# One program part for cross-attention and experts, with the experts' first work placed in the last output projection

## The chip, the cores and the metric

The kernel runs on one core of a Trainium2 chip. The metric is the device time of one execution in microseconds (us), given as the median of several runs. TensorE (PE) multiplies and transposes, with its weight loads shown apart (PEld); VectorE (DVE), ScalarE (ACT) and GpSimd (POOL) do the elementwise work; SyncE (SP) issues nearly all DMAs. Engines meet only at semaphores.

## The reference

One decoder layer over 4096 tokens (two sequences of 2048) of width 512, in float32:

```
x = x + attn(layernorm(x))            # scores against 2048 fixed keys per head, squared relu, no softmax
x = x + xattn(layernorm(x), ctx)      # 16 heads of 64, 128 context rows a batch, mask, softmax, then Wo
x = x + ffn(layernorm(x))

ffn(x): shared = (silu(x @ sg) * (x @ su)) @ sd                  # 512 -> 1024 -> 512, every token
        e, s   = argmax(x @ gate_w), sigmoid(max(x @ gate_w))    # one of 32 experts
        routed = expert_e(x * s)                                 # the same form, weights of expert e
        return shared + routed
```

Every layernorm needs mean and variance of its 512 numbers per token.

## The kernel before

Products in full float32 precision are made from two halves: each operand is a rounded high part H and a remainder L, and a product is three matmuls, H·H + H·L + L·H (split_matmuls, lines 47 to 49). So whatever goes to PE, weights or activations, is first copied by ACT to the high part, and then DVE subtracts that from the source to get the low part.

Tokens lie in 32 tiles of 128 rows, and 8 groups of 4 tiles (GT = 4, GROUPS = 8). The kernel is a row of program parts ("blocks"). Each has its own program for each engine, and the engines meet at the end of a part, before the next begins: self-attention; the preparation of cross-attention (keys, values, query and output weights); cross-attention proper (lines 645 to 992); the experts (line 1202 on).

Cross-attention proper goes through the 8 groups, with 8 head pairs (steps j = 0 to 7) in each, 64 steps in all. A step is: query, scores, mask, exponentials, normalization by GpSimd (probabilities), transposes of the probabilities (p_transpose), their split by ACT and DVE (t_high, t_low), product with the values (values), and the split of that (a_high, a_low). Steps are staggered: in step n PE makes the scores of n, then the values of n-2 and the transposes of n-1. A finished group is multiplied with the output weights in step 1 of the next group: project(g, i) for tile i, 8 pairs of 3 matmuls each, 24 in all, into the PSUM banks pY0 and pY1 in turn. DVE adds x1, which SP has loaded into xr (add), computes the tile's statistics (out_stats), and SP stores the sum as x2. Within PE's program of the last group, nothing is left to do after p_transpose of step 62; behind the loop come values(62), p_transpose(63), values(63) and then the four projections of the last group (lines 988 to 992).

The experts' part begins with GpSimd's constants, three small conversions on DVE, and the layernorm statistics of all 32 tiles (layernorm_stats, line 489: 32 aggregations and a chain of 15 small operations, each of which waits for the one before). SP loads the router weight rw, the first x2 tiles (xb) and the shared weights. These come in twelve parts of 512 KB: 0 to 3 the gate weight, 4 to 7 the up weight, 8 to 11 the down weight. They pass through a staging tile with three slots (split_weights, lines 453 to 486): part n is loaded when part n-3 has been split, `wait(sp, low_done, n + 1 - SLOTS)`; ACT copies it (high), DVE subtracts (low). The first four tiles are normalized (norm), transposed by PE (x_transpose), copied and subtracted (x_high, x_low), one after another through one PSUM bank, pX.

Then the shared experts run group by group (shared, lines 1332, 1517 and 1678): 8 chunks i of 128 hidden columns, each 12 matmuls of gate, 12 of up; ACT makes the sigmoid, DVE two products and the subtraction, ACT the copy; in chunks 0 and 1 PE adds the router's logits and their transposes. Then four down projections of 24 matmuls. PE starts group 0 when all four tiles are subtracted (xL) and the gate weight is split, the first up matmul when all 8 first parts are (`low_done` 8), and the first down projection when all 12 are. In group 0 the down weight's parts are copied and split in chunks 1, 3, 5 and 7, behind the chunk's own hidden values. After that come the routed experts.

An engine works through its program strictly in the order written, SP too: a DMA behind a waiting one is not issued.

Of the kernel before, what the change touches and what calls it, by code (L numbers as in the profile page):

```python
# [11 lines left out]
NB = 2  # L12
KC = C // P
# [475 lines left out]
def layernorm_stats(nc, link, stats, parts, mv, var, tmp, rstd, mybir):  # L489

    ALU = mybir.AluOpType
    n = stats.shape[1]
    for t in range(n):
        m = nc.vector.bn_aggr(out=mv[:, t, :], in_=stats[:, t, 0:parts, :])
    link(m)
    link(nc.vector.tensor_scalar(var[:, :], mv[:, :, 1], EPS, None, ALU.add))
    rsqrt(nc, link, rstd[:, :], tmp[:, :], var[:, :], ALU, mybir.dt.int32)


def cross_attention(nc, ident, stats, x1, ctx_in, mask, Wq, Wk, Wv, Wo, x2, mybir, bass, ExitStack):  # L500
# [17 lines left out]
    with ExitStack() as keep:  # L518
        sbk = lambda n, s, d=F32: keep.enter_context(nc.sbuf_tensor("b_" + n, s, d))

        kH, kL = (sbk(n, [P, NPAIR, 2, KEYS], F32R) for n in ("kH", "kL"))
        later = [nc.dram_tensor(f"later{n}", (P, NPAIR, KEYS), F32, kind="Internal").ap() for n in "HL"]
        vH, vL = (sbk(n, [KEYS, NB, NPAIR, 2, P], F32R) for n in ("vH", "vL"))
        wqH, wqL = (sbk(n, [P, KC, INNER], F32R) for n in ("wqH", "wqL"))
        woH, woL = (sbk(n, [P, NPAIR, C], F32R) for n in ("woH", "woL"))


        with ExitStack() as ctx:
            sb = lambda n, s, d=F32: ctx.enter_context(nc.sbuf_tensor("b_" + n, s, d))
            ps = lambda n, s: ctx.enter_context(nc.psum_tensor("b_" + n, s, F32))  # L530
            wkH, wkL = (sb(n, [P, KC, INNER], F32R) for n in ("wkH", "wkL"))
            wvH, wvL = (sb(n, [P, KC, INNER], F32R) for n in ("wvH", "wvL"))
            cx = sb("cx", [KEYS, NB, C])
            cH, cL = (sb(n, [P, KC, NB, KEYS], F32R) for n in ("cH", "cL"))
            k1 = [sb(n, [P, 2, KEYS], F32R) for n in ("k1H", "k1L")]
            pC = [ps(f"pC{i}", [P, 2, NB, KEYS]) for i in range(2)]
            pK = [ps(f"pK{i}", [P, NB, KEYS]) for i in range(2)]
            pV = [ps(f"pV{i}", [KEYS, NPAIR // 2, 2, HD]) for i in range(2)]
            s = {n: ctx.enter_context(nc.semaphore("bs_" + n)) for n in
                 "c_in zero ct cH cL k_ps kH kL k_out0 k_out1 v_ps vH vL".split()}  # L540
            parts = []
            for w, hi, lo in ((Wk, wkH, wkL), (Wv, wvH, wvL), (Wq, wqH, wqL)):
                w_v = w.rearrange("(a p) n -> p a n", p=P)
                parts += [(w_v[:, a, :], hi[:, a, :], lo[:, a, :]) for a in range(KC)]
            wo_v = Wo.rearrange("(a p) n -> p a n", p=P)
            parts += [(wo_v[:, a:a + 2, :], woH[:, a:a + 2, :], woL[:, a:a + 2, :]) for a in range(0, NPAIR, 2)]
            load, high, low, low_done = split_weights(nc, ctx, "bs_", parts, mybir)
            block = ctx.enter_context(nc.Block())

            @block.sync  # L550
            def _(sp):
                sp.dma_start(cx[:, :, :], ctx_in.rearrange("b k c -> k b c")).then_inc(s["c_in"], 16)
                load(sp)

            @block.gpsimd
            def _(pool):
                nc.gpsimd.memset(kH[:, :, :, :].bitcast(F32), 0.0).then_inc(s["zero"], 1)
                nc.gpsimd.memset(kL[:, :, :, :].bitcast(F32), 0.0).then_inc(s["zero"], 1)
                nc.gpsimd.memset(vH[:, :, :, :, :].bitcast(F32), 0.0).then_inc(s["zero"], 1)
                nc.gpsimd.memset(vL[:, :, :, :, :].bitcast(F32), 0.0).then_inc(s["zero"], 1)  # L560
                for j in range(NPAIR):
                    pool.wait_ge(s["kL"], j + 1)
                    for part, dst in zip(k1, later):
                        pool.dma_start(dst[:, j, :], part[:, j % 2, :].bitcast(F32)).then_inc(s[f"k_out{j % 2}"], 16)
                for i in range(2):
                    pool.wait_ge(s[f"k_out{i}"], 32 * NPAIR // 2)

            @block.scalar
            def _(act):
                copy = lambda out, in_: nc.scalar.activation(out, in_, ACT.Copy)  # L570
                for i in range(2):
                    act.wait_ge(s["ct"], i + 1)
                    copy(cH[:, 2 * i:2 * i + 2, :, :], pC[i][:, :, :, :]).then_inc(s["cH"], 1)
                high(act, 0, KC)
                act.wait_ge(s["zero"], 2)
                for j in range(NPAIR):
                    high(act, KC + j // 2, KC + (j + 1) // 2)
# [41 lines left out]
            def _(pe):  # L619
                pe.wait_ge(s["c_in"], 16)  # L620
                for a in range(KC):
                    for b in range(NB):
                        m = nc.tensor.transpose(pC[a // 2][:, a % 2, b, :], cx[:, b, a * P:(a + 1) * P], ident[:, :])
                    if a % 2:
                        m.then_inc(s["ct"], 1)
# [1178 lines left out]
```

## Time and profile before

| | us |
|---|---|
| median of 3 runs | 2952.77 (2951.02 to 2953.56) |
| profiled execution, its own time | 2952.46 |
| its span | 2950.8 |
| PE busy | 2813.2 |
| DVE busy | 1788.2 |
| ACT busy | 1599.4 |
| POOL busy | 1027.5 |

The span runs from the first to the last instruction that the profiler recorded; the execution's own time holds a little more than the span. Times inside the trace count from the start of the span. "Idle before" on a row is the time for which the engine had stood still when this instruction began, and behind the arrow stands what it had waited for. The granted clock is a share of full speed; 1.00 is 2.4 GHz and 0.50 is 1.2 GHz.

### The profile page before, as it was taken

The page shows a single profiled execution, that of the slowest core. Times are in us where ns is not written, and L with a number is a line of the kernel's source. Part 1 is how long each engine was busy: PE and PEld are TensorE (multiplying, and loading weights), DVE is VectorE, ACT ScalarE, POOL GpSimd, SP SyncE. Part 2 cuts the span into 40 slices and gives each one's busy share as a digit, 9 for nine tenths or more (in the row PEclk, how much of TensorE's full clock was granted, in tenths as well). Part 3 has the DMA queues.
Part 4 walks back from the last instruction along what each step waited for, and adds up shares of the span by engine and source line. Part 5 has one row for each costly group of instructions (what it writes and reads, how often), then busy time and mean ns, then how long its engine had stood idle before and what let it go on. Part 6 is the DMA issues. An engine that isn't in the chain of part 4 may idle for free. (4 is left out here: it accounts for less than half of the span.)

```text
span 2950.8 us, 46232 instructions
## 1 busy us (share of the span) xinstructions
PE 2813.2 (95%) x13287; PEld 2296.6 (78%) x13289; DVE 1788.2 (61%) x2726; ACT 1599.4 (54%) x2755; POOL 1027.5 (35%) x705
## 2 busy tenths in 40 slices
PE   7999999999779999999969999999999999999998
PEld 5888888888558777777747888887788888888886
DVE  6566665665465566666544443444877864776776
ACT  6888878887545555555522111111465753665665
POOL 5888888888611122221200000000133322332332
PEclk9999999999889999999979999999999999999999
DMA  1000000000320111111031111121888873876885
GB/s 61 26 26 11 25 28 25 25 11 11 111 75 30 43 36 47 36 40 43 29 115 65 57 57 57 58 73 40 285 311 288 307 273 118 285 265 228 290 284 181
DMA packets 185544, 322.71 MB, mean 109 GB/s; under 512 B 23657, under 2 KB 42089, under 8 KB 185473
## 3 DMA queue, kind: packets, MB, share of 16 engines
q1 hardware_dynamic: 173680, 295.56, 29.2%
q0 software_dynamic: 11792, 26.25, 2.6%
q8 instruction: 38, 0.62, 0.1%
q14 instruction: 34, 0.27, 0.0%
HBM read 286.86 MB, written 46.66 MB: 113 GB/s over the span
## 5 line engine op out<-in xcount | busy, mean ns | idle before, releaser
L156 POOL TENSOR_TENSOR a_pL<-a_p,a_pH 128x1024 fp32r<-128x1024 f32 x256 | 615.2, 2405 | 151.0 <-DVE a_p L344 149.3
L344 DVE TENSOR_TENSOR a_p<-a_r,a_pS 128x1024 f32<-128x1024 f32 x256 | 312.5, 1221 | 282.1 <-ACT a_r L163 275.8
L1058 DVE TENSOR_TENSOR e_wL<-e_raw,e_wH 128x1024 fp32r<-128x1024 f32 x384 | 451.0, 1222 | 36.2 <-PE d_pU L1732 23.8
L1053 ACT CAST e_wH<-e_raw 128x1024 fp32r<-128x1024 f32 x384 | 384.4, 1053 | 86.6 <-PE d_pD L49 58.7
L735 POOL TENSOR_TENSOR b_S<-b_S,b_ri 128x512 f32<-128x512 f32 x128 | 133.2, 1040 | 528.7 <-DVE b_ri L831 528.7
L163 ACT ACTIVATE a_r<-a_pS 128x1024 f32<-128x1024 f32 x256 | 262.2, 1024 | 100.0 <-PE a_pS L49 95.4
L163 ACT ACTIVATE a_pH<-a_r 128x1024 fp32r<-128x1024 f32 x256 | 272.0, 1062 | 9.0
L1273 POOL DMA_INDIRECT out<-d_og,c_iw x46 | 90.9, 1976 | 356.5 <-DVE d_og L1620 356.5
L47 PE MATMUL a_pS<-a_qH,a_kH 128*128 (+1 forms) x512 | 206.0, 402 | 0.6 <-DVE a_p L344 0.6
L47 PE MATMUL a_pO<-a_pH,a_vH 128*128 128x512 f32 x512 | 201.9, 394 | 0.6 <-POOL a_pL L156 0.6
L48 PE MATMUL a_pS<-a_qL,a_kH 128*128 (+1 forms) x512 | 202.0, 395 | 0.0
L49 PE MATMUL a_pO<-a_pH,a_vL 128*128 128x512 f32 x512 | 201.8, 394 | 0.0
L48 PE MATMUL a_pO<-a_pL,a_vH 128*128 128x512 f32 x512 | 201.8, 394 | 0.0
L49 PE MATMUL a_pS<-a_qH,a_kL 128*128 (+1 forms) x512 | 200.0, 391 | 0.0
L752 ACT ACTIVATE b_S<-b_S,b_nm 128x128 f32<-128x128 f32 x512 | 198.5, 394 | 1.8 <-DVE b_nm L826 1.3
L1268 POOL MEMSET d_xg<- 128x512 f32 x1 | 0.5, 527 | 535.2 <-PE c_pR L1653 535.2
L747 ACT ACTIVATE b_qH<-b_pQ 128x512 fp32r<-128x512 f32 x64 | 38.4, 600 | 248.2 <-PE b_pQ L49 248.2
L1381 ACT CAST d_hH<-d_pT 128x512 fp32r<-128x512 f32 x92 | 54.0, 587 | 194.4 <-PE d_pT L1743 194.4
L1732 PE MATMUL d_pG<-e_wH,d_xH 128*128 128x512 f32 x370 | 153.1, 414 | 2.6 <-DVE e_wL L1058 1.6
L47 PE MATMUL d_pD<-e_wH,d_hH 128*128 128x512 f32 x368 | 147.5, 401 | 0.0
L1732 PE MATMUL d_pG<-e_wL,d_xH 128*128 128x512 f32 x370 | 145.1, 392 | 0.0
L1732 PE MATMUL d_pU<-e_wH,d_xH 128*128 128x512 f32 x370 | 144.8, 391 | 0.0
(296 smaller groups left out, 7171.0 us busy)
## 6 DMA issues: line engine op xcount, KB each, us to landing
e_raw<-in_L_ffn_routed_gate_w SPq DMA_DIRECT2D x256, 256.0 KB, 4.5
e_raw<-in_L_ffn_routed_up_w SPq DMA_DIRECT2D x256, 256.0 KB, 5.6
e_raw<-in_L_ffn_routed_down_w SPq DMA_DIRECT2D x128, 512.0 KB, 6.7
a_xb<-in_x SPq DMA_DIRECT2D x8, 1024.0 KB, 5.7
x<-a_o SPq DMA_DIRECT2D x32, 256.0 KB, 2.3
b_xb<-x SPq DMA_DIRECT2D x32, 256.0 KB, 2.7
b_xr<-x SPq DMA_DIRECT2D x32, 256.0 KB, 3.0
x<-b_xr SPq DMA_DIRECT2D x32, 256.0 KB, 2.5
```

The costliest lines, as they stand in the source:

```text
L47: nc.tensor.matmul(out, a[0], b[0], start=first, stop=False)
L48: nc.tensor.matmul(out, a[0], b[1], start=False, stop=False)
L49: return nc.tensor.matmul(out, a[1], b[0], start=False, stop=last)
L156: nc.gpsimd.tensor_tensor(pL[:, j % RING, :, :], p[:, j % 2, :, :], pH[:, j % RING, :, :].bitcast(F32), ALU.subtract).then_inc(s["low"], 1)
L163: return nc.scalar.activation(out, in_, func)
L344: v.tensor_tensor(p[:, j % 2, :, :], r[:, j % 2, :, :], pS[j % 2][:, :, :], ALU.mult).then_inc(s["p"], 1)
L735: nc.gpsimd.tensor_tensor(S[at], S[at], ri[at].unsqueeze(2).to_broadcast([P, HALF, KEYS]), ALU.mult).then_inc(s["prob"], 1)
L752: e = nc.scalar.activation(S[:, j % 2, i, :], S[:, j % 2, i, :], ACT.Exp, bias=nm[:, j % 2, i:i + 1], accum_out=rs[:, j % 2, i:i + 1])
L1053: copy(self.wH[n][:, :, :], self.raw[n][:, :, :]).then_inc(self.s["high"], 1)
L1058: unit.tensor_tensor(self.wL[n][:, :, :], self.raw[n][:, :, :], self.wH[n][:, :, :].bitcast(self.F32), self.sub).then_inc(self.s["low"], 1)
L1273: pool.indirect_dma_start(bounds_check=bound, oob_is_err=False, **how).then_inc(count, 16)
L1732: m = nc.tensor.matmul(bank[half][:, :], x[:, a, :], w[n][:, j, :], start=first, stop=last)
```

## The change

Cross-attention proper has no part of its own any more: cross_attention returns its five engine programs as functions, and feed_forward calls them at the start of its own. The tiles of both now lie at fixed offsets from one start, so that both can be in memory at once; the experts' statistics, one-hot table and indices get places that cross-attention doesn't use. The last group's projections and the experts' first work are written as one sequence for each engine ("ending"). Of GpSimd, the constants come right after its last product. The core of the diff:

```diff
-def layernorm_stats(nc, link, stats, parts, mv, var, tmp, rstd, mybir):
+def layernorm_stats(nc, link, stats, parts, mv, var, tmp, rstd, mybir, lo=0, hi=TILES):   # tiles lo to hi only
...
 cross-attention, DVE, in step j:
+                if j == 1 and last:
+                    aside()
                 if j == 1 and not first:
                     outputs(g - 1)
...
 cross-attention, PE, behind the loop:
-                values(n - 2, NB - 1, NPAIR - 2)
-                p_transpose(n - 1, NPAIR - 1)
-                values(n - 1, NB - 1, NPAIR - 1)
-                for i in range(GT):
-                    project(GROUPS - 1, i)
+        g = GROUPS - 1
+        wait(pe, s["res"], GT * g)
+        project(g, 0, range(NPAIR - 2))
+        values(n - 2, NB - 1, NPAIR - 2)
+        project(g, 1, range(NPAIR - 2))
+        p_transpose(n - 1, NPAIR - 1)
+        values(n - 1, NB - 1, NPAIR - 1)
+        project(g, 0, range(NPAIR - 2, NPAIR))
+        project(g, 1, range(NPAIR - 2, NPAIR))
+        ending(project)
...
 experts, SP:
+        def ending(reload, store, free):
+            sp.wait_ge(b["score"], QUERIES)
+            load(0, 0)
+            load(1, 1)
+            sp.dma_start(rw[:, :, :], gate_w.rearrange("(a p) n -> p a n", p=P)).then_inc(s["g_in"], 16)
+            load_parts(sp, 0, 3)
+            reload(GROUPS - 1, 0)
+            reload(GROUPS - 1, 1)
+            for i in range(2, GT):
+                sp.wait_ge(s["normed"], i - 1)
+                load(i, i)
+            load_parts(sp, 3, 6)
+            store(TILES - 4, 0)
+            reload(GROUPS - 1, 2)
+            load_parts(sp, 6, 2 * KC)
+            store(TILES - 3, 1)
+            reload(GROUPS - 1, 3)
+            store(TILES - 2, 2)
+            store(TILES - 1, 3)
+            for i in range(GT - 2, GT):
+                free(GROUPS - 1, i)
+        cross["sync"](sp, ending)
+        load_parts(sp, 2 * KC)
...
 experts, ACT (x_high and x_low of the first four tiles read the banks pG0, pG1, pU0, pU1 in place of pX):
+        cross["scalar"](act)
+        act.wait_ge(b["q_ps"], QUERIES)
+        high_parts(act, 0, 2)
         act.wait_ge(s["g_in"], 16)
         nc.scalar.activation(rH, rw[:, :, :], ACT.Copy).then_inc(s["rH"], 1)
+        high_parts(act, 2, KC)
+        x_high(0, 0)
+        high_parts(act, KC, KC + 2)
+        x_high(1, 1)
+        x_high(2, 2)
+        high_parts(act, KC + 2, 2 * KC)
+        x_high(3, 3)
...
 experts, DVE:
+        def aside():
+            dve.wait_ge(b["seen"], KNOWN)          # KNOWN = TILES - 2 * GT = 24
+            link = Link(dve, s["own"])
+            layernorm_stats(nc, link, stats, 1, mv, var, tmp, rstd, mybir, 0, KNOWN)
+        def ending(t_low, a_low, add, out_stats):
+            g, t = GROUPS - 1, TILES - GT
+            dve.wait_ge(b["tp"], QUERIES)
+            norm(0, 0)
+            norm(0, 1)
+            t_low(QUERIES - 1)
+            a_low(QUERIES - 1, QUERIES // GROUPS - 1)
+            add(g, 0)
+            norm(0, 2)
+            low_parts(dve, 0, 1)
+            add(g, 1)
+            norm(0, 3)
+            low_parts(dve, 1, 2)
+            x_low(0, 0)
+            out_stats(g, 0)
+            low_parts(dve, 2, 3)
+            out_stats(g, 1)
+            low_parts(dve, 3, 4)
+            x_low(1, 1)
+            x_low(2, 2)
+            add(g, 2)
+            low_parts(dve, 4, 5)
+            out_stats(g, 2)
+            dve.wait_ge(s["rH"], 1)
+            v.tensor_tensor(rL, rw[:, :, :], rH.bitcast(F32), ALU.subtract).then_inc(s["rL"], 1)
+            low_parts(dve, 5, 7)
+            x_low(3, 3)
+            add(g, 3)
+            low_parts(dve, 7, 8)
+            out_stats(g, 3)
...
 experts, DVE, shared, in chunk i:
+                if first and i == 6:
+                    dve.wait_ge(b["seen"], TILES)
+                    layernorm_stats(nc, step, stats, 1, mv, var, tmp, rstd, mybir, KNOWN, TILES)
...
 experts, PE:
+        def ending(project):
+            g = GROUPS - 1
+            x_transpose(0, 0)
+            project(g, 2)
+            x_transpose(1, 1)
+            x_transpose(2, 2)
+            project(g, 3)
+            x_transpose(3, 3)
+        cross["tensor"](pe, ending)
...
 PE, logits and logit_transposes of group 0 (their banks are those of pY0 and pY1):
+            if isinstance(g, int) and g == 0:
+                pe.wait_ge(b["res"], TILES - 1)    # TILES for the transposes
```

The project of the changed kernel takes a range of head pairs; it waits for the split attention output (aL) up to pair 5 at its start, and singly for pairs 6 and 7. The matmuls are the same and as many as before.

## Rows read from the trace of the kernel before

**Rows 1.** The page, section 1: busy us, share of the span, instructions of each engine.

```profile
PE 2813.2 (95%) x13287; PEld 2296.6 (78%) x13289; DVE 1788.2 (61%) x2726; ACT 1599.4 (54%) x2755; POOL 1027.5 (35%) x705
```

**Rows 2.** Busy us of PE, PEld, DVE, ACT, POOL by stage; PE's granted clock, DMA.

```profile
1460.00:1480.00 20.00, 12.75 (x51) 10.14 (x49) 8.67 (x12) 10.61 (x38) 4.16 (x4) 0.78 0.00 1
...
1505.00:1530.00 25.00, 4.38 (x16) 2.86 (x16) 14.45 (x63) 7.00 (x10) 1.38 (x10) 0.50 0.57 193
```

**Rows 3.** Timeline of PE, end of cross-attention: start, us, instruction, [idle before <- releaser].

```profile
1463.74 0.50 PE L47 MATMUL b_pO<-b_tH,b_vH 128*128 128x512 f32 x1 [2.10 <-DVE b_tL L793]
...
1466.07 1.81 PE L933 MATMUL b_pT<-ident,b_S 128*128 128x128 f32 x8
...
1477.16 0.50 PE L47 MATMUL b_pO<-b_tH,b_vH 128*128 128x512 f32 x1 [2.37 <-DVE b_tL L793]
...
1481.39 0.39 PE L49 MATMUL b_pY<-b_woH,b_aL 128*128 128x512 f32 x1
...
1502.38 0.39 PE L49 MATMUL b_pY<-b_woH,b_aL 128*128 128x512 f32 x1
```

**Rows 4.** Timeline of PE, start of the shared experts.

```profile
1514.95 1.12 PE L1630 MATMUL c_pX<-ident,c_x 128*128 128x128 f32 x4 [12.18 <-DVE c_x L1403]
...
1530.60 0.79 PE L47 MATMUL c_pG<-c_xH,c_wgH 128*128 128x512 f32 x1 [1.41 <-DVE c_xL L1397]
...
1535.46 0.61 PE L49 MATMUL c_pG<-c_xH,c_wgL 128*128 128x512 f32 x1
...
1537.65 0.50 PE L47 MATMUL c_pU<-c_xH,c_wuH 128*128 128x512 f32 x1 [1.59 <-DVE c_wuL L484]
```

**Rows 5.** Timelines of ACT and DVE, last step of cross-attention.

```profile
1474.83 1.02 ACT L759 ACTIVATE b_tH<-b_pT 128x1024 fp32r<-128x1024 f32 x1 [0.93 <-PE b_pT L933]
...
1479.56 0.60 ACT L764 ACTIVATE b_aH<-b_pO 128x512 fp32r<-128x512 f32 x1 [3.71 <-PE b_pO L49]
...
1480.19 0.69 DVE L793 TENSOR_TENSOR b_aL<-b_pO,b_aH 128x512 fp32r<-128x512 f32 x1 [3.08 <-ACT b_aH L764]
```

**Rows 6.** Chain of work that ended last, 1500 to 1540: start, us, what.

```profile
1516.52 3.31 DMA c_stage<-in_L_ffn_shared_gate_w
...
1532.05 3.21 DMA c_stage<-in_L_ffn_shared_up_w
```

**Rows 7.** The staging tile of the shared weights; durations in ns, minimum/median/maximum.

```profile
L478 ACT ACTIVATE c_wgH<-c_stage x4: 1056/1057/1060, 1511.8 to 1519.9; 128x1024 fp32r<-128x1024 f32 x4
...
L484 DVE TENSOR_TENSOR c_wgL<-c_stage,c_wgH x4: 1218/1218/1225, 1515.3 to 1520.9; 128x1024 fp32r<-128x1024 f32 x4
...
DMA to landing us min/median/max: 3.2/4.5/7.0
```

**Rows 8.** Timeline of DVE, start of the shared experts.

```profile
1508.74 2.22 DVE L494 BATCH_NORM_AGGREGATE c_mv<-stats 128x2 f32<-128x6 f32 x32
...
1514.35 1.00 DVE L1403 TENSOR_SCALAR c_x<-c_xb,c_mv,c_rstd 128x512 f32<-128x512 f32 x2
...
1522.08 0.69 DVE L1397 TENSOR_TENSOR c_xL<-c_pX,c_xH 128x512 fp32r<-128x512 f32 x1
```

**Rows 9.** Timeline of DVE, second step of the last group of cross-attention.

```profile
1410.51 0.69 DVE L845 TENSOR_TENSOR b_xr<-b_pY,b_xr 128x512 f32<-128x512 f32 x1 [2.17 <-PE b_pY L49]
...
1416.11 0.69 DVE L845 TENSOR_TENSOR b_xr<-b_pY,b_xr 128x512 f32<-128x512 f32 x1 [4.91 <-PE b_pY L49]
1416.72 0.68 DVE L850 BATCH_NORM_STATS2 stats<-b_xr 128x6 f32<-128x512 f32 x1
```

**Rows 10.** Timelines of DVE and PE, first shared group, chunks 6 and 7.

```profile
1577.28 0.69 DVE L1397 TENSOR_TENSOR c_hL<-c_h,c_hH 128x512 fp32r<-128x512 f32 x1 [0.70 <-ACT c_hH L1344]
...
1579.19 0.69 DVE L1521 TENSOR_TENSOR c_sg<-c_sg,c_pG 128x512 f32<-128x512 f32 x1 [1.22 <-ACT c_sg L1337]
...
1581.34 0.69 DVE L1533 TENSOR_TENSOR c_h<-c_sg,c_pU 128x512 f32<-128x512 f32 x1 [1.46 <-PE c_pU L49]
...
1584.95 0.80 PE L47 MATMUL c_pD<-c_wdH,c_hH 128*128 128x512 f32 x1 [3.27 <-DVE c_wdL L484]
```

More of the change, by code:

```diff
@@ L517, in cross_attention @@
     x2_t = x2.rearrange("(t p) c -> p t c", p=P)
[L518 to L564, printed above, removed]
-                for i in range(2):
[L566 to L570, printed above, removed]
-                for i in range(2):
[L572 to L577, printed above, removed]
-                    act.wait_ge(s["k_ps"], j + 1)
@@ new lines, in body, with gpsimd @@
+                        sp.dma_start(dst[row, :, i, :].bitcast(F32), part[row, :, :]).then_inc(s["k_in"], 16)
+            if not first:
+                outputs(g - 1)
+            if not last:
+                for i in range(GT):
+                    sp.wait_ge(s["normed"], g * GT + GT + i - 1)
+                    load(g * GT + GT + i, i)
+        groups(sp, body)
+        ending(reload, store, free)
+    def gpsimd(pool):
+        def body(g, b, pb, first, last):
+            for j in range(NPAIR):
+                n = NPAIR * g + j
+                for half in range(2):
+                    at = (slice(None), j % 2, slice(half * HALF, (half + 1) * HALF))
+                    pool.wait_ge(s["rinv"], 2 * n + half + 1)
+                    nc.gpsimd.tensor_tensor(S[at], S[at], ri[at].unsqueeze(2).to_broadcast([P, HALF, KEYS]), ALU.mult).then_inc(s["prob"], 1)
+        groups(pool, body)
@@ L995 @@
+    return {"sync": sync, "gpsimd": gpsimd, "scalar": scalar, "vector": vector, "tensor": tensor, "s": s, "steps": NPAIR * GROUPS}
 class Place:
@@ new lines, in feed_forward @@
+    starts, ends = c.at(c.end, "starts", [EXP, EXP], BF), c.at(c.end, "ends", [EXP, EXP], BF)
+    ix, iw = (c.at(c.end, n, [P, 1], I32) for n in ("ix", "iw"))
+    first_silu = c.at(c.end, "first", [1, 1], F32)
+    before = c.at(c.end, "before", [P, TILES + 1, EXP], BF)
+    table = c.at(c.end, "table", [1, 3, NSLOT], I32)
+    assert c.end <= 201 * KB + 64, c.end / KB
+    mv = c.at(201 * KB + 256, "mv", [P, TILES, 2], F32)
+    rstd, var, tmp = (c.at(c.end, n, [P, TILES], F32) for n in ("rstd", "var", "tmp"))
@@ new lines, in feed_forward @@
+    s = {n: ctx.enter_context(nc.semaphore("c_" + n)) for n in
+         ("const g_in rH rL x_in0 x_in1 r_in0 r_in1 normed xt xH xL gate up sig gated h hH hL logit_ps lt logit top own score xs xs_out"
+          " down sum out0 out1").split()}
+    rs = {n: ctx.enter_context(nc.semaphore("r_" + n)) for n in
+          "step counted blocks ranked placed indexed index table".split()}
+    ds = {n: ctx.enter_context(nc.semaphore("d_" + n)) for n in
+          "zero ix ib iw x_in b_in turn xt xH xL silu h ht hH hL used sum".split()}
```

1975 lines of the change are left out of this document (988 added, 987 removed).

## The prediction

> **What bounds the kernel now.** I read the page first: TensorE is busy for 95% of the span [rows 1], so only the places where it is not busy, or not at full clock, are worth anything. The table by stage then shows where such a place lies at the seam between cross-attention and experts: PE is busy 12.75 of 20 us at a mean granted clock of 0.78 from 1460 to 1480, and 4.38 of 25 us at 0.50 (the 1.2 GHz level) from 1505 to 1530 [rows 2]. The timeline of PE gives the seam in detail. The last projection matmul starts at 1502.38 [rows 3]; the first transpose for the experts starts at 1514.95 after 12.18 us of idleness; the first gate matmul starts at 1530.60, its twelve matmuls run at (1535.46 - 1530.60)/11 = 0.44 us each, and the first up matmul follows at 1537.65, after a wait for the last split weight, at full clock [rows 4]. At full clock one such matmul takes (1502.38 - 1481.39)/90 = 0.233 us [rows 3]. From 1537.65 on PE runs without a gap that this change touches, up to the first down projection. So I compute when the changed kernel starts that first up matmul, and compare with 1537.65. All times are on the clock of the profiled execution before: span 2950.8, its own time 2952.46 us, 0.3 under the median of the runs shown (2952.77).
>
> **The tail of cross-attention.** PE ends the transposes of step 62 at 1466.07 + 1.81 = 1467.9 [rows 3]. What they need from there is the same, but now 18 of the 24 matmuls of projections 0 and 1 fill the two waits for the split probabilities. Steps of PE:
> - Projection 0, 18 matmuls. The clock is low here (the eight transposes take 1.81 us). A steady stretch took 4.2 us to reach full clock from 1477.16 [rows 3] and 5 to 7 us from 1530.60 [rows 4]; I take 1471: 7 slow (3.1), 11 fast (2.6), end 1473.6.
> - Values of step 62, 6 fast: 1475.0. Projection 1, 18 fast (4.2): 1479.2. Transposes of step 63, half of 1.81 at full clock: 1480.2.
> - Wait for the split of step 63: 2.4, as the 2.37 of before [rows 3]. DVE now does two normalizations first, but these take 1.00 [rows 8] beside ScalarE's copy of 1.02 [rows 5], for which DVE had to wait anyway, so they cost nothing; their input is loaded with parts 0 to 2 (below). PE resumes at 1482.6.
> - Values of step 63, 6 matmuls. After a wait of 2.10 the clock fell in the trace (the 1.81 us transposes behind it) [rows 3], so I take 2.3 us, not 1.4: 1484.9. The attention halves are ready about 1.5 later: copy 0.60 and subtraction 0.69 with handovers [rows 5]: 1486.4. Before, 21 matmuls of projection 0 covered this; now three do, a new wait of about a microsecond. The last three (1.3 slow): projection 0 ends at 1487.7, projection 1 at 1490.3.
> - Transposes of four tiles (about 0.5 each), projections 2 and 3 (5.6 each): PE is through at about 1503.4, as late as before in spite of the filled waits, since the x transposes are new here.
>
> **The weights set the start of the experts.** The staging ring has three slots: part n is loaded only when part n-3 has been split. Parts 0 to 2 are issued when the last scores are done, at 1461.6 (the 2.10 before 1463.74 [rows 3]), and at the longest landing, 7.0 [rows 7], are there by 1472. But nothing is split before DVE has come past the add of tile 28, and ScalarE keeps the copies of x behind the copies of weights, DVE its subtractions in the order written. First split (low 0): 1487.7 + 0.8 (add) + 0.5 (norm) + 1.2 = 1490.2. From there three round trips follow one another. Prices: load to landing 3.3 (3.31 and 3.21 in the chain [rows 6]; the row of the ring gives 3.2 at least, 4.5 median, 7.0 at most), copy 1.06, subtraction 1.22 [rows 7], x copy 0.60 [rows 5], x subtraction and add 0.69, statistics 0.68 [rows 8, 9]; back to back DVE loses some 0.1 less on each.
> - Trip 1, part 3: issue 0.1, landing 3.3, copy 1.06, then x copy 0 (0.6), x subtraction 0 (0.7), statistics 28 (0.7), low 2 (1.2): 7.6, to 1497.8.
> - Trip 2, part 5: 0.1 + 3.3 + 1.06, x copy 1 (0.6), x subtractions 1 and 2 (1.4), add 30 (0.7), low 4 (1.2): 8.3, to 1506.1.
> - Trip 3, part 7: 0.1 + 3.3 + 1.06, x copy 3 (0.6), x subtraction 3 (0.7): 5.8, to 1511.9.
> PE, through at 1503.4, waits 8.5 us for that last subtraction. Then twelve gate matmuls at 1.2 GHz (PE was idle, as before 1530.60): 5.3, and the first up matmul at 1517.2. The add of tile 31 waits for its reload, which SP issues only after part 7 and the landing of a store. Both are half a part's size; at 3.3 each they end 6.6 behind 1506.2, at 1512.8 at the latest, and low 7, behind this add, at 1514.7, still before 1517.2: the wait of 1.59 for it [rows 4] goes. The logits and their transposes wait for these adds, and start later than that. Gain at this point: 1537.65 - 1517.2 = 20.4 us. The block end and start, the constants, the 32-tile aggregation (2.22 + 3.4 [rows 8]) are all inside this difference.
>
> **The two halves of the statistics.** Tiles 0 to 23 in the last group: 24/32 of 2.22, plus the linked chain from 1510.96 to 1514.35, 3.4 [rows 8]: 5.1 us on DVE, while PE does projections of group 6. Before, DVE idled 2.17 before the first add there and 4.91 before the second [rows 9]; the first add comes 2.9 late, but PE needs it only at the third projection, 5.6 after the second has begun. Cost nothing; without this cover it would be 5.1. Tiles 24 to 31 in chunk 6 of the first shared group: 0.6 + 3.4 = 4.0 on DVE, behind the subtraction that ends at 1577.97; the next product of DVE was due at 1579.19 and comes at 1582.0, the hidden product then at 1582.8 instead of 1581.34, and from it hangs the copy and split of the last down weight, for which PE waited till 1584.95 [rows 10]. Here nothing covers: 1.4 us lost. Bounds: 0, if the last part could be split without that product (the order of the queues excludes it), and 2.8, the full delay of the product. I take 1.4, the chain of these rows.
>
> The new placement of tiles, one program part less to start, GpSimd's constants right after its last product: no row prices a placement; I take nothing, bounds -2 to +2, about what the runs shown differ by among themselves (2951.02 to 2953.56).
>
> Sum: 2952.46 - 20.4 + 1.4 = 2933.5 us; on the median it would be 0.3 more, which I leave in the rounding. Forecast **2933.5**.
>
> **The rivals.**
> - The ring is slower than a single load: the loads meet other traffic (part 4, reloads and stores are issued 0.4 to 2.3 us apart). At the median of 4.5 instead of 3.3 three trips cost 3.6 more, at 5.1 5.4: 2937 to 2939. For it speaks that only loads with little behind them took 3.3; against it, that the ones in these trips are mostly alone too.
> - The clock stays low. The trace shows short waits keeping PE down (0.78 from 1460 to 1480 [rows 2]), and the changed order has waits at 1480 and 1485. If projections 2 and 3 run at 0.44 (48 matmuls, 10 us more), PE is through at 1513.4, the x copy and subtraction of tile 3 follow (1.5), the gate starts at 1514.9: 3.0 later, 2936.5. [...]
> - The weights don't bind. Then the gate starts 1.5 after PE is through, at 1504.9, at full clock (2.8): up at 1507.7, gain 30 less 1.4: 2924. Each trip would have to be 2 to 3 us shorter; 3.2 as the least landing speaks against it.
> - Slower than before: the idleness of 8.5 us leaves PE at 1.2 GHz not only for the gate but on through the first shared group. Each matmul costs 0.21 more; it decides from 19.0/0.21 = 90 matmuls on. Over all 288 of the group, less the 12 counted, it is 58 us: 2991. Against it: PE came back within 7 us from 1530.60 after a worse gap [rows 4].
> - The early work doesn't get early (SP stuck behind a reload, say), and the order of before is kept: 2953.
>
> **How the numbers follow.** Forecast 0.66, own range 2929 to 2937 (the bounds of the statistics, +-2 of the placement, 1 of the clock). Slow ring 0.14, low clock 0.07, weights not binding 0.06, slower 0.04, nothing 0.03. For 8 in 10 the range is 2927 to 2941. This kernel tells 0.2%, 6 us, from no change: faster 0.93, same 0.03, slower 0.04.
>
> **What would show it.** In the profile after: first up matmul of the shared experts about 20 us earlier relative to the last scores; the copy of part 3, 5 and 7 each preceded by idleness of ScalarE for a load; PE idle some 8 us between the last x transpose and the first gate matmul, whose wait is for the subtraction of tile 3; gate matmuls at 0.44; the wait before the first down projection 1.4 longer than 3.27 [rows 10]; the adds of group 6 late without a gap on PE. Wrong it would be if PE starts the gate right behind its last transpose, if projections 2 and 3 show 0.44, or if anything behind the first shared group changes its length by more than 2 us.

## The result, and the profile after

| | before | after |
|---|---|---|
| median of the runs, us | 2952.88 (2951.02 to 2953.56, 4 runs) | 2922.49 (2921.37 to 2924.04, 4 runs) |
| profiled execution, us | 2952.46 | 2923.17 |
| its span, us | 2950.8 | 2921.5 |
| mean granted clock of TensorE | 0.982 | 0.985 |

The ratio is 0.9903, with a 95% interval of 0.989 to 0.9915. The forecast was 2933.5 us in a range of 2927 to 2941: the direction was right, but the time lies 11.0 us below the forecast, outside the range.

TensorE does the same matmuls in less time. The page of the kernel after, section 1, against [rows 1]:

```profile
PE 2803.1 (96%) x13288; PEld 2296.0 (79%) x13289; DVE 1788.9 (61%) x2741; ACT 1598.8 (55%) x2755; POOL 1065.4 (36%) x705
```

Its busy time fell from 2813.2 to 2803.1, for one instruction more. A change that only moves work about should not do that, except by the clock. Where those 10 us went is asked below, after the seam. The same stages as in [rows 2], after (the columns are the same):

```profile
1460.00:1480.00 20.00, 17.41 (x74) 13.72 (x73) 6.15 (x10) 8.85 (x25) 3.38 (x12) 0.88 0.32 112
1480.00:1505.00 25.00, 14.15 (x70) 11.64 (x69) 15.21 (x20) 9.35 (x12) 0.00 (x0) 0.88 0.47 143
1505.00:1530.00 25.00, 25.00 (x104) 19.62 (x104) 13.22 (x27) 6.09 (x11) 0.00 (x0) 0.92 0.32 110
```

From 1505 to 1530 PE is now busy for 25.00 us of 25, where it was 4.38. Its timeline through the seam, after (start, us, instruction, [idle before <- releaser]), answers to [rows 3] and [rows 4]:

```profile
1455.07 0.28 PE L49 MATMUL b_pS<-b_kH,b_qL 128*128 128x256 f32 x1
...
1474.60 0.59 PE L47 MATMUL b_pO<-b_tH,b_vH 128*128 128x512 f32 x1 [2.37 <-DVE b_tL L783]
...
1478.73 0.50 PE L47 MATMUL b_pY<-b_woH,b_aH 128*128 128x512 f32 x1 [0.22 <-DVE b_aL L783]
...
1493.20 0.60 PE L1684 MATMUL c_pU<-ident,c_x 128*128 128x128 f32 x4
1504.64 0.80 PE L47 MATMUL c_pG<-c_xH,c_wgH 128*128 128x512 f32 x1 [10.85 <-DVE c_xL L1421]
...
1509.51 0.39 PE L47 MATMUL c_pU<-c_xH,c_wuH 128*128 128x512 f32 x1
```

The last scores start at 1455.07 and the first up matmul at 1509.51, 54.4 us later. In the kernel before, the last scores are

```profile
1461.37 0.28 PE L49 MATMUL b_pS<-b_kH,b_qL 128*128 128x256 f32 x1
```

and it was 76.3 us (1537.65 of [rows 4] less 1461.37). TensorE is through with the last x transpose at 1493.8 and then waits 10.85 us for the last x subtraction. ScalarE's timeline shows what that subtraction stood behind, after:

```profile
1485.38 1.06 ACT L478 ACTIVATE c_wgH<-c_stage 128x1024 fp32r<-128x1024 f32 x1 [4.39 <-DMA c_stage<-in_L_ffn_shared_gate_w]
...
1493.23 1.06 ACT L478 ACTIVATE c_wuH<-c_stage 128x1024 fp32r<-128x1024 f32 x1 [4.53 <-DMA c_stage<-in_L_ffn_shared_up_w]
...
1502.32 1.06 ACT L478 ACTIVATE c_wuH<-c_stage 128x1024 fp32r<-128x1024 f32 x1 [3.27 <-DMA c_stage<-in_L_ffn_shared_up_w]
1503.29 0.58 ACT L1342 ACTIVATE c_xH<-c_pU 128x512 fp32r<-128x512 f32 x1
```

These are the copies of parts 3, 5 and 7, each after idleness that a load ends, and the x copy behind the last of them. VectorE's timeline has the two ends of this chain, the first split of a weight and the last subtraction of x, after:

```profile
1480.79 1.22 DVE L484 TENSOR_TENSOR c_wgL<-c_stage,c_wgH 128x1024 fp32r<-128x1024 f32 x1
...
1503.90 0.69 DVE L1421 TENSOR_TENSOR c_xL<-c_pU,c_xH 128x512 fp32r<-128x512 f32 x1 [2.34 <-ACT c_xH L1342]
```

Now the parts of the 29.3 us by which the span is shorter, from the starts of four instructions in both traces: up to the last scores 6.4; from there to the first up matmul 21.8; from there to the last shared down matmul -0.9 (566.8 became 567.7); the routed experts behind it 2.0 (846.3 became 844.3). PE's busy time fell by 6.2 us between the first bias (849.5) and the last scores, and by 5.1 from there to the first up matmul, where fewer of its matmuls and transposes ran at the lower clock; the rest is +1.2. The first item stands in no step of the forecast: it lies in the loop of cross-attention, whose instructions the change does not touch. One tile's instructions over the loop show it. The mask bias is made once a group, eight times; durations are in ns, minimum/median/maximum, and then first and last start in us. Before:

```profile
L817 DVE TENSOR_SCALAR b_bias<-b_mu x8: 426/427/429, 849.5 to 1394.0; 128x512 f32 x5, 128x512 f32<-128x512 uint8 x3
```

After:

```profile
L807 DVE TENSOR_SCALAR b_bias<-b_mu x8: 427/427/429, 849.6 to 1388.6; 128x512 f32 x5, 128x512 f32<-128x512 uint8 x3
```

The first comes at the same time, the last 5.4 earlier: 544.5 us became 539.0. VectorE and ScalarE take as long for each instruction as before. The matmuls do not. The output projections in the kernel before:

```profile
L47 PE MATMUL b_pY<-b_woH,b_aH x256: 393/394/628, 918.3 to 1501.9; 128*128 128x512 f32 x128
...
L48 PE MATMUL b_pY<-b_woL,b_aH x256: 392/394/628, 918.6 to 1502.1; 128*128 128x512 f32 x128
```

and after:

```profile
L47 PE MATMUL b_pY<-b_woH,b_aH x256: 389/389/632, 918.0 to 1492.5; 128*128 128x512 f32 x128
...
L48 PE MATMUL b_pY<-b_woL,b_aH x256: 387/389/632, 918.3 to 1492.7; 128*128 128x512 f32 x128
```

394 ns against 389 is small, and the same form on the same tiles. The distance from one start to the next (the pitch), which is what a busy engine pays, tells it better. I took its mean over all neighbouring matmuls into the same output tile, at full clock: b_pY 233.3 ns before and 227.0 after, b_pQ 232.3 and 229.3, b_pO 230.1 and 227.5. In the shared experts it is 226.6 to 229.3 in both kernels, in self-attention 229.3 to 233.3 in both.

### The profile page after: what moved, and what is told of

It reads as the page before. It is cut to its first block, busy times and chain, and to the rows that moved or that the text cites. A ratio compares the mean times of both kernels' runs of the same rounds, so it can differ in the third digit from the quotient of the medians.

```text
span 2921.5 us, 46250 instructions
## 1 busy us (share of the span) xinstructions
PE 2803.1 (96%) x13288; PEld 2296.0 (79%) x13289; DVE 1788.9 (61%) x2741; ACT 1598.8 (55%) x2755; POOL 1065.4 (36%) x705
## 4 chain that ended last, share of the span: by engine, by line
PE 53%; issue 11%; DVE 3%; POOL 2%; ACT 2%; DMA 1%; ACTq 0%; DVEq 0%; POOLq 0%; SPq 0%
PE d_pG L1798 8%; PE d_pU L1798 8%; PE d_pD L49 3%; PE d_pD L47 3%; PE d_pD L48 3%; POOL b_S L727 2%; PE c_pD L47 2%; PE c_pD L49 2%; PE c_pD L48 2%; PE c_pG L47 2%; PE c_pG L49 2%; PE c_pG L48 2%; PE c_pU L47 2%; PE c_pU L49 2%; PE c_pU L48 2%
## 5 line engine op out<-in xcount | busy, mean ns | idle before, releaser
L163 ACT ACTIVATE a_r<-a_pS 128x1024 f32<-128x1024 f32 x256 | 262.3, 1024 | 100.1 <-PE a_pS L49 95.4
L1290 POOL DMA_INDIRECT out<-d_og,c_iw x46 | 123.7, 2689 | 340.4 <-DVE d_og L1672 340.4
L1368 ACT ACTIVATE c_hH<-c_h 128x512 fp32r<-128x512 f32 x64 | 40.5, 632 | 192.4 <-DVE c_h L1582 192.4
```

The source lines that it names most:

```text
L163: return nc.scalar.activation(out, in_, func)
L1290: pool.indirect_dma_start(bounds_check=bound, oob_is_err=False, **how).then_inc(count, 16)
```

## The experiments

What differs for these matmuls is where their tiles lie. The change gave cross-attention fixed offsets on a base of its own. Before, its weights, keys and values lay 128 bytes past a multiple of 256 and x and q 0 past one, t and a 192; after, all lie at 128. In the shared experts all large tiles lie at one remainder in both kernels (224 and 128). A matmul reads two tiles, a stationary one (its weight load, PEld in the profile) and a moving one. So theory A: a matmul is quickest when its stationary and its moving tile have the same remainder. Theory B: something else in the merging of the two parts.

**1. All tiles of the kernel before brought to one remainder.**

```diff
+            sb("pad0", [P, 96])
             mu = sb("mu", [P, ROWT, KEYS], U8)
...
             nm, rs, ri = (sb(n, [P, 2, SUB]) for n in ("nm", "rs", "ri"))
+            sb("pad1", [P, 208])
             tH, tL = (sb(n, [KEYS, 2, GTOK], F32R) for n in ("tH", "tL"))
```

> The kernel before, with 384 unused bytes per partition ahead of the x tiles of cross-attention and 832 ahead of tH, so that every large tile of that part lies at the same remainder (640 bytes) modulo 1024, as they do in the kernel after; before, x, q and S lay at 256 and t and a at 448, the weights, values and keys at 640. No instruction changes. Theory A (the 6.3 us that the cross-attention loop gained come from where the stationary and the moving tile of a matmul lie to each other): the 512-column matmuls of b_pY, b_pO and b_pQ go from 231-233 ns apart to 227-230, the group period from 81.06 to 80.2 us, the time to 2946.5 us (2945 to 2948). Theory B (it comes from something else that the change did in this part: its merging with the experts, the joint weight code, other semaphores): pitch 233 ns, period 81.06, time 2952.9 us.

2945.27 us (10 runs) against 2952.12 (19 runs of before), ratio 0.9977 (0.9967 to 0.9986): 6.9 us, by the interval 4 to 10, from unused bytes alone. The loop, in the trace of this kernel:

```profile
L819 DVE TENSOR_SCALAR b_bias<-b_mu x8: 426/427/429, 847.1 to 1386.1; 128x512 f32 x5, 128x512 f32<-128x512 uint8 x3
```

539.0 us, exactly the loop of after, and each pitch as there within 0.3 ns. From the last bias to the last scores it takes 66.6 us, where it was 67.4 before and 66.5 after, and from the last scores to the first up matmul 76.4 us, as before. Theory B falls; the 6.4 us are the placement's.

**2. Only aH and aL moved, to four distances from the output weights.** One line in each, with 48, 16, 112 or 176 columns of padding:

```diff
+            sb("pad1", [P, 48])
             aH, aL = (sb(n, [P, NPAIR, GTOK], F32R) for n in ("aH", "aL"))
```

> The kernel before with 192 unused bytes ahead of aH and aL alone, which puts them at the same remainder modulo 1024 (640) as the output weights woH and woL; q, x, t and S stay where they were. Theory A: only b_pY changes, from 233.3 to 227 ns apart; 8 groups of 96 output matmuls at 0.0063 us are 4.8 us, so 2948.1 us (2947 to 2949.5), and b_pO, b_pQ keep their 231-233 ns. Theory A2 (an absolute address or the whole layout matters, not the two tiles to each other): b_pO or b_pQ change with it, or b_pY does not. Theory B: 2952.9 us and nothing changes.

> The kernel before with 64 unused bytes ahead of aH and aL: they come to 512 modulo 1024, 128 away from the output weights (640), where they were 192 away before. Read from the pitch of the b_pY matmuls alone. Theory A with a step of 64 or 128 bytes: 227 ns, as with equal remainders, and some 2948 us. Theory A with a coarser step (256 bytes and more): still 233 ns and 2952.9 us.

> The kernel before with 448 unused bytes ahead of aH and aL: they come to 896 modulo 1024, 256 away from the output weights (640). Read from the pitch of the b_pY matmuls. If equal remainders modulo 256 are enough: 227 ns, time some 2947 to 2948 us. If it takes 512 or more: 233 ns, 2952 us. If the absolute remainder of 640 was what helped in the earlier run: 233 ns.

> The same with 704 unused bytes: aH and aL come to 128 modulo 1024, 512 away from the output weights. If equal remainders modulo 256 or 512 are enough: 227 ns for b_pY, some 2947 to 2948 us. If it takes 1024: 233 ns, 2952 us.

And with another 64 bytes ahead of the output weights, so that these and a lie at the same remainder, but at another one:

```diff
+        sbk("pad0", [P, 16])
         woH, woL = (sbk(n, [P, NPAIR, C], F32R) for n in ("woH", "woL"))
...
+            sb("pad1", [P, 48])
             aH, aL = (sb(n, [P, NPAIR, GTOK], F32R) for n in ("aH", "aL"))
```

> The kernel before with 64 unused bytes ahead of the output weights and 192 ahead of aH and aL: both come to 704 modulo 1024 (192 modulo 256), equal to each other but not to the 640 (128 modulo 256) of the earlier runs; x and q come to 64 and t to 0 modulo 256 where wq, k and v stay at 128. Theory A (the two tiles to each other): b_pY 227 ns, b_pQ and b_pO at 231 to 233 as before, loop 541.1 us in place of 544.5, 2948 us. Theory A2 (each tile's own place counts, 128 modulo 256 is a good one): b_pY 233 ns or more, loop 544.5, 2952 us.

| kernel | a and wo, modulo 1024 | start to start, b_pY, ns | loop, us | time, us |
|---|---|---|---|---|
| before | 448, 640 | 233.3 | 544.5 | 2952.1 |
| a + 64 bytes | 512, 640 | 233.2 | 544.3 | 2951.3, one run |
| a + 192 | 640, 640 | 226.9 | 541.1 | 2946.98, ratio 0.9985 (0.9975 to 0.9995) |
| a + 448 | 896, 640 | 226.9 | 541.2 | 2947.3, one run |
| a + 704 | 128, 640 | 226.9 | 541.1 | 2943.4, one run |
| both moved | 704, 704 | 227.2 | 541.8 | 2947.2, one run |
| all tiles aligned | 640, 640 | 226.8 | 539.0 | 2945.3 |

One line of each kind; in the trace with 64 bytes, which changed nothing:

```profile
L47 PE MATMUL b_pY<-b_woH,b_aH x256: 390/393/474, 917.8 to 1499.4; 128*128 128x512 f32 x128
```

and in the trace of a + 448:

```profile
L47 PE MATMUL b_pY<-b_woH,b_aH x256: 389/389/628, 917.4 to 1496.8; 128*128 128x512 f32 x128
```

For b_pY a distance of 0, 256 or 512 bytes (modulo 1024) gives 227 ns, one of 128 or 192 gives 233. It is the distance that counts and not the place: at 704 the pair is as quick as at 640. In that run, with both moved, x, q and t came to other unequal distances, and b_pQ rose from 232.3 to 233.4, b_pO from 230.1 to 232.5. The time of a + 192 is 5.1 us less, where 8 x 96 x 0.0064 = 4.9 were to be had. The 2943.4 of a + 704 is not the placement's: its loop is as long as that of a + 192, but this one execution was 2.9 us quicker from the last scores to the first up matmul (73.4 us), and in it no matmul behind the wait ahead of the first down projection ran at the lower clock.

**3. TensorE's old order at the end of cross-attention, in the kernel after.**

```diff
-        wait(pe, s["res"], GT * g)
-        project(g, 0, range(NPAIR - 2))
         values(n - 2, NB - 1, NPAIR - 2)
-        project(g, 1, range(NPAIR - 2))
         p_transpose(n - 1, NPAIR - 1)
         values(n - 1, NB - 1, NPAIR - 1)
-        project(g, 0, range(NPAIR - 2, NPAIR))
-        project(g, 1, range(NPAIR - 2, NPAIR))
+        wait(pe, s["res"], GT * g)
+        project(g, 0)
+        project(g, 1)
```

> The kernel after with TensorE's old order at the end of cross-attention: the last values, transposes, values, and then the output projections of the first two tiles in one piece, in place of projections cut in two around the transposes. The first gate matmul of the experts should not move if the ring of three staging buffers for the weights sets it: TensorE ends its last x transpose later by about the 4 to 5 us of projection work that no longer fills the two waits for t_low and a_low, but it had 10.9 us of idle time there; 2922.5 us, within 1. If TensorE's own order binds, it is 4 to 5 us slower: 2927.

2923.53 us, ratio 0.9904 (0.9888 to 0.9921) against 0.9903. PE's timeline in this kernel:

```profile
1453.63 0.28 PE L49 MATMUL b_pS<-b_kH,b_qL 128*128 128x256 f32 x1
...
1496.62 0.60 PE L1682 MATMUL c_pU<-ident,c_x 128*128 128x128 f32 x4
1504.63 0.80 PE L47 MATMUL c_pG<-c_xH,c_wgH 128*128 128x512 f32 x1 [7.42 <-DVE c_xL L1419]
```

The gate matmul starts at the same time of the trace to 0.01 us, but that is luck: the last scores of this execution are 1.4 us earlier (1453.63 against 1455.07). Counted from them, the last x transpose is 4.9 us later (43.0 in place of 38.1), the wait ahead of the gate 3.4 shorter, and the gate 1.4 later (51.0 in place of 49.6). So most of what TensorE lost was covered by its wait, as expected of the ring; a part was not. VectorE's timeline shows where 0.8 of it comes from:

```profile
1479.08 0.69 DVE L835 TENSOR_TENSOR b_xr<-b_pY,b_xr 128x512 f32<-128x512 f32 x1 [5.61 <-PE b_pY L49]
...
1480.14 1.22 DVE L484 TENSOR_TENSOR c_wgL<-c_stage,c_wgH 128x1024 fp32r<-128x1024 f32 x1
```

The first split stands behind the add of the first projection, which ends later in this order: it ends 27.7 us behind the last scores in place of 26.9. The other 0.6 lie in the three round trips. In four traces with the cut projections, after's among them, the gate stands at 48.4 to 49.6. So the cutting, a large part of the diff, is worth some 1.4 to 2.6 us by single traces, and 1.0 by the medians, which the intervals don't tell from nothing; it is not the 4 to 5 us by which TensorE's work moved.

**4. The first weight parts split earlier, in the kernel after.** On each engine the split goes between the last steps of cross-attention; parts 4 to 7 follow where parts 0 to 3 were, and SP issues parts 3 to 5 before the x loads that wait.

```diff
         n = NPAIR * GROUPS            # ScalarE
+        split(0, 2)
         a_high(n - 2, GROUPS - 1, NPAIR - 2)
+        split(2, 3)
         t_high(n - 1)
+        split(3, 4)
         a_high(n - 1, GROUPS - 1, NPAIR - 1)
...
+        split(0, 1)                   # VectorE
         a_low(n - 2, NPAIR - 2)
+        split(1, 3)
         ending(t_low, a_low, add, out_stats)
...
             t_low(QUERIES - 1)
+            low_parts(dve, 3, 4)
             a_low(QUERIES - 1, QUERIES // GROUPS - 1)
...
+            load_parts(sp, 3, 6)      # SyncE
             for i in range(2, GT):
                 sp.wait_ge(s["normed"], i - 1)
                 load(i, i)
-            load_parts(sp, 3, 6)
```

> The kernel after with the first weight parts of the shared experts split earlier: high 0 and 1 on ScalarE before a_high of the second to last step, high 2 behind it, high 3 behind the last t_high; low 0 on VectorE before the second to last a_low, low 1 and 2 behind it, low 3 behind t_low; SP issues parts 3 to 5 ahead of the x loads that wait, stores tile 28 before part 7. Theory A (the ring of three staging buffers sets the first gate matmul, as the prediction said): low 0 ends at about 1467 in place of 1482, part 3 is issued there, the ring runs out by 1488, and then the last x transpose on TensorE (1493.2) binds: the gate starts at 1495 to 1497 in place of 1504.6, with less idle time ahead of it and so less of it at the lower clock: 9 to 11 us faster than the kernel after, 2911 to 2914 us. Rival (the x tiles and the residual reloads bind as well, or the DMAs take longer when they are issued during the last projections): gate at 1502 to 1504, 2920 to 2922 us.

2910.39 us (4 runs), ratio 0.9862 (0.9844 to 0.9879): 12.1 less than the kernel after. VectorE's first split of a weight in this trace:

```profile
1463.46 1.43 DVE L484 TENSOR_TENSOR c_wgL<-c_stage,c_wgH 128x1024 fp32r<-128x1024 f32 x1 [0.77 <-ACT c_wgH L478]
```

and TensorE's side of it:

```profile
1453.66 0.28 PE L49 MATMUL b_pS<-b_kH,b_qL 128*128 128x256 f32 x1
...
1489.76 0.60 PE L1692 MATMUL c_pU<-ident,c_x 128*128 128x128 f32 x4
1491.78 0.50 PE L47 MATMUL c_pG<-c_xH,c_wgH 128*128 128x512 f32 x1 [1.41 <-DVE c_xL L1431]
...
1494.63 0.39 PE L47 MATMUL c_pU<-c_xH,c_wuH 128*128 128x512 f32 x1
```

The first split starts 17.3 us earlier in the trace, 15.9 counted from the last scores, and the wait ahead of the gate falls from 10.85 to 1.41 us, the copy and subtraction of the last x tile. The rival falls. From the last scores to the first up matmul it is 41.0 us where it was 54.4. Two of these 13.5 us are the clock: the twelve gate matmuls take 1494.63 - 1491.78 = 2.85 in place of 1509.51 - 1504.64 = 4.87. By stage, in this kernel:

```profile
1460.00:1480.00 20.00, 16.91 (x80) 13.52 (x79) 13.73 (x18) 12.13 (x22) 3.61 (x12) 1.00 0.62 207
1480.00:1505.00 25.00, 23.59 (x111) 18.59 (x110) 12.68 (x22) 6.34 (x9) 0.00 (x0) 1.00 0.39 134
```

The granted clock is 1.00 throughout, the upper level, where the kernel after had 0.88. That is this execution's: in the trace of experiment 6, which has the same edit, the matmuls behind a wait of 2.37 us ran at the lower clock, and from the last scores to the first up matmul it took 42.2 us.

**5. Self-attention's p tiles brought to the remainder of its keys and values, in the kernel after.** Keys, values and q lie 128 past a multiple of 256 and p, pH and pL 64; 144 columns bring these to 128, and 160, the control, to 192; the tiles behind them, oT and o1, move along.

```diff
+        sb("pad", [P, 144])
         r, p = sb("r", [P, 2, 2, GTOK]), sb("p", [P, 2, 2, GTOK])
```

> The kernel after with 576 unused bytes ahead of r and p of self-attention, so that r, p, pH and pL lie at the same remainder modulo 1024 (640) as kH, kL, vH, vL, qH, qL. No instruction changes. If the same rule holds there, the value matmuls of a_pO (pH against vH, 448 bytes apart before) go from 233.2 to about 227 ns apart, while the score matmuls (equal remainders already, 229 to 232 ns) stay: 8 groups of 4 heads of 48 value matmuls are 1536, at 0.0062 us 9.5 us, as TensorE is 100% busy there: 2913 us (2911 to 2917). If the score and the value matmuls, which alternate there, get their pitch from something else, nothing changes: 2922.5 us.

> The kernel after with 640 unused bytes ahead of r and p of self-attention, 64 more than in the run that gained 11.8 us: p, pH and pL come to 192 modulo 256, where kH, vH and q are at 128. Theory A (equal remainders modulo 256 of the two tiles of a matmul): the value matmuls are back at 233 ns, and the time at 2921 to 2923 us. Rival (the gain came from the larger gap or from any move of these tiles): 227 ns, 2911 us.

The aligned one took 2910.72 us, ratio 0.986 (0.9843 to 0.9878), 11.8 less than the kernel after. The control took 2919.8 in one run. The value matmuls of self-attention, first and last start, in the kernel after:

```profile
L49 PE MATMUL a_pO<-a_pH,a_vL x512: 392/394/403, 34.7 to 769.3; 128*128 128x512 f32 x171
```

with 144 columns:

```profile
L49 PE MATMUL a_pO<-a_pH,a_vL x512: 388/389/398, 34.8 to 757.2; 128*128 128x512 f32 x171
```

and with 160:

```profile
L49 PE MATMUL a_pO<-a_pH,a_vL x512: 392/392/399, 32.5 to 766.8; 128*128 128x512 f32 x171
```

From first to last they take 734.6, 722.4 and 734.3 us. The control gives most of it back, not all: in it the stage began 2.2 us earlier, but in the traces that began as early with p at its old place (32.3 to 33.0) it took 736.1 us, and whenever it began it ended at 768.4 to 769.5. The control ends at 766.8, about 2 us before them, the aligned one at 757.2, 12 before. So equal remainders are what helps here too, and the rival (any move, or the larger gap) falls. The value matmuls went from 233.3 to 227.1 and 231.0 ns, where the expectation had 233 for the control. The score matmuls, whose own two tiles were equal all along, went from 230.8 to 227.5 ns (mean of their three kinds) when p moved, and to 231.6 in the control. So the place of tiles that a matmul does not read has a part in it; which of those that moved it is, was not tried.

The 231.0 has its place when the distance is taken with its sign, the address of the moving tile less that of the stationary one, modulo 256. In the projections a is stationary and wo moves; in the value matmuls v is stationary and p or t moves; in the query matmuls wq is stationary and x moves. At 0 all traces have 226.8 to 229.3 ns. At 64 it is 230.1 (b_pO before) and 231.0 (a_pO in the control), at 128 it is 232.3 (b_pQ before), 232.5 (b_pO, both moved) and 233.2 (b_pY, a + 64), at 192 it is 233.3 (b_pY and a_pO before) and 233.4 (b_pQ, both moved). These are readings of runs made for other questions, of different forms; no run was made to test this order.

**6. Both together.** The edits of 4 and 5 in one kernel.

> The kernel after with both edits that gained alone: the first weight parts split early (2910.4 us alone, 12.1 less than the kernel after) and 576 unused bytes ahead of r and p of self-attention (2910.7 alone, 11.8 less). They touch stages that do not overlap (self-attention ends at about 770 us, the split begins at 1450 us), so the gains should add: 2898.6 us, within 1.5. If a part of either came from something they share, for instance the time at which the chip lowers and raises TensorE's clock, the sum falls short: 2901 to 2908.

2898.44 us (2897.11 to 2899.22, 5 runs), ratio 0.9821 (0.9808 to 0.9834), where 2898.6 was expected. The two gains add up, and this version beats both kernels: 53.6 us less than before, against 30.4 for the change itself.

**7. The late statistics behind the second down projection, in the kernel after.**

> The kernel after with the layernorm statistics of tiles 24 to 31 moved from chunk 6 of the first shared group to behind its second down projection's sum. Read from the trace: first up matmul to first down matmul was 47.3 us in the kernel before and 48.2 after, where the prediction took 1.4 for these statistics. If they cost what was said, it is 47.3 again and the wait ahead of the first down matmul is gone with it; the place where they now are has VectorE ahead of TensorE or delays x_low of the second group, up to 1 us. Time 2921.5 to 2922.5 us. If the 0.9 us comes from the down weights that arrive later against the chunks, it stays 48.2.

First up to first down matmul: 47.3 us before, 48.14 after (48.13 to 48.17 in the five other traces with the statistics in this place), 47.18 here. The wait ahead of the first down matmul, after:

```profile
1557.65 0.79 PE L47 MATMUL c_pD<-c_wdH,c_hH 128*128 128x512 f32 x1 [4.24 <-DVE c_wdL L484]
```

and here:

```profile
1505.96 0.39 PE L47 MATMUL c_pU<-c_xH,c_wuH 128*128 128x512 f32 x1
...
1553.14 0.80 PE L47 MATMUL c_pD<-c_wdH,c_hH 128*128 128x512 f32 x1 [3.27 <-DVE c_wdL L484]
```

The wait is back at the 3.27 of [rows 10], not gone as expected. The statistics cost 0.97 us where the change put them, and nothing that can be seen in the other place. Up to the last shared down matmul this trace is even 2.3 us shorter than that of after (565.4 against 567.7). The other 1.3 are the clock: behind the wait of 3.3 to 4.2 us the first matmuls of the down projection run at the lower level, 12 in the kernel after and 6 here, at 0.21 us more each. How many they are changes between traces whose wait is the same: behind 3.27 us it was 11 in the kernel before and none with a + 704 (granted clock 1.00 there). The whole kernel took 2919.9 in one run, too little to tell a microsecond by.

## Why the prediction was wrong, point by point

**The step that failed** is "the new placement of tiles ...: no row prices a placement; I take nothing, bounds -2 to +2". It was worth 6.4 us, 6.9 when measured by itself. Alone it takes the sum to 2927.1, the edge of the range; the other 4.6 us down to 2922.49 are small misses on the same side: 1.4 at the seam, 0.5 at the statistics, 2.0 in the routed experts and 0.7 between the profiled execution and the median. The bounds were taken from the scatter of the runs, which says nothing of the price of an edit. A row to bound it by was at hand: the same form of matmul ran 233 ns apart in [rows 3] and 227 apart in the shared experts of the same trace (c_pG 227.4, c_pU 226.7). Over the 8 x (96 + 96 + 48) = 1920 projection, query and value matmuls of the loop those 6 ns are 12 us at most, and a bound of that size belonged in the range. The Trainium skill would not have warned either: SBUF — State Buffer, "SBUF: two separate sides", says that TensorE's reads wait for nobody, and TensorE: Matmul & The Clock Gate, "Step-by-step: what each phase is for", that loading the next weights takes nothing from the running matmul. By these two sentences placement would be worth nothing; the runs measured 6.9 and 11.8 us.

**The seam was right in its mechanism.** I count from the last scores, so that the faster loop drops out; of each pair the first is the forecast: end of the first split 28.8 and 26.9; three round trips 21.7 (7.6, 8.3, 5.8) and 22.6; gate matmul 50.5 and 49.6; its twelve matmuls 5.3 and 4.9 (0.43 each up to 1508.65, 0.23 from 1509.05 on: the clock rose in between); first up matmul 55.8 and 54.4. Gain 20.4 and 21.8. The 1.4 between them is within what executions differ by: from the last scores to the first up matmul the traces of kernels with the seam of before have 73.4 to 76.4 us, those with the seam of after 53.1 to 54.4. That the ring sets the start is shown from both sides, by experiment 3 (PE 4.9 later, gate only 1.4) and 4 (ring earlier, gate 38.1 in place of 49.6 us behind the last scores). The loads took 3.3 to 3.8 us as [rows 6] had them.

**TensorE's end was too pessimistic by 3.** Through with the transposes 42.0 after the last scores in the forecast, 38.7 measured: the clock was up 6.8 us behind the last scores in place of 9.6, the projections ran at 227 ns, and the wait for the attention halves was 0.22 where about 1 was taken. The earlier end cost and brought nothing at the gate, as the ring was later; but projection 0, too, ended 1.7 earlier than forecast, and the first split, behind its add, came at 26.9 in place of 28.8.

**The statistics.** The first half was free, as said: from the last bias to the last scores it took 66.5 us with it and 66.6 in experiment 1 without it. The second cost 0.97 where 1.4 was taken: aggregation and chain took 3.7 us (1549.6 to 1553.3) in place of 4.0, and the hidden product behind them came 0.9 later in its chunk than in the kernel before, in place of 1.5.

**The routed experts** came out 2.0 shorter in the profiled execution, which no step had. In the traces of six other kernels that share that part with the kernel after it is 845.6 to 846.9, in those of six that share it with the kernel before 846.0 to 847.4, so that most of the 2.0 is the scatter of single executions.

**The rivals.** Slow ring: no, 22.6 against 21.7. The clock stays low: no. Behind the wait of 2.37 us the matmuls from 1474.60 to 1478 run at 0.43 us, at the lower level, but from 1479.07 on the projections run at 0.228, at the upper one. The lower level comes back at the gate, behind 10.85 us of idleness, and experiment 4 got those 2 us back. "The weights don't bind", at 2924, was nearest in time and wrong in its reason: TensorE did wait for 10.85 us. A time that fits a rival is no evidence for it while a stage elsewhere has changed.

The sum closes: 2933.5 less 6.4 (placement), 1.4 (seam), 0.5 (statistics, 0.9 up to the last shared down matmul in place of 1.4) and 2.0 (routed) is 2923.2, the profiled execution's 2923.17.

## What to carry to other kernels

When an edit moves tiles, compare the distance between starts of one form of matmul across the stages of the trace you have: if stages differ, placement has a price, and a few unused bytes that bring stationary and moving tiles to equal remainders modulo 256 are the cheapest edit to try. When work is pulled forward through a small ring of buffers, the time of its first release counts, and how well the engine in front is filled counts only as far as it moves that release: find who releases the first slot and move that. Ask of every "no row prices this" whether two rows that differ without a reason already do.

## What the hardware showed that I had not expected

- At full clock the pitch of a 128x512 fp32r matmul, each with its own weight load, depends on where its tiles lie: for b_pY 227 ns at a distance of 0, 256 or 512 bytes modulo 1024, 233 at 128 or 192, for the same instructions (experiments 1 and 2). With its sign, moving less stationary modulo 256, the distance puts all four forms in one order, 227 to 229 at 0, 230 to 231 at 64, 232 to 233 at 128, 233 at 192 (experiment 5). Over a stage in which TensorE never rests this is 1.7% of its time (734.6 against 722.4 us).
- Tiles that a matmul does not read take part in it: the score matmuls of self-attention changed between 227.5 and 231.6 ns as r, p, pH, pL, oT and o1 moved, and the query matmuls of cross-attention stay at 229.3 with all remainders equal. Which accesses meet there, TensorE's own two or those of the three other engines, was not tried, and stays open.
- Behind one and the same wait (3.27 us before the first down projection) TensorE ran 11 matmuls at the lower clock in the trace of one kernel, 6 in another and none in a third: 2.3 us of scatter at one place, as large as some of the effects looked for here.
